# A four-layer graph network on one core: where the layer steps stand among the attention groups, the bank of the projection, and two node buffers instead of a copy

## The reference

```python
# layers 0, 2, 3: normalised adjacency times nodes times a 128x128 weight, plus bias (0 and 2 add the identity to adj)
x = _layernorm(x + (d[:, :, None] * adj * d[:, None, :]) @ x @ W + b)
# layer 1: additive attention
q = x @ WQ; k = x @ WK
score = einsum('bijd,d->bij', relu(q[:, None] + k[:, :, None]), p)
x = _layernorm(x + softmax(score + mask(adj > 0)) @ x)
```

## Time and profile before

| | |
|---|---|
| median of 3 runs | 13884.19 us (13881.76 to 13884.51) |
| the profiled execution, first to last instruction | 13883.0 us |
| busy share of the span | DVE 96%, PE 93%, ACT 93%, POOL 8% |
| a middle sweep, from its first mask to the next sweep's | 1699.6 us |

### The profile page before, as it was taken

The page is one execution under the profiler, slowest core; times in us unless marked ns, Lnnn a source line. Parts: engine busy times, 40 slices in busy tenths (PEclk is TensorE's granted clock), DMA queues, the critical chain, the costliest instruction groups (busy, mean ns, idle before and its releaser), DMA issues.

```text
span 13883.0 us, 318102 instructions
## 1 busy us (share of the span) xinstructions
PE 12956.7 (93%) x143877; PEld 5442.7 (39%) x143877; DVE 13327.1 (96%) x14041; ACT 12942.7 (93%) x8528; POOL 1095.3 (8%) x706
## 2 busy tenths in 40 slices
PE   7889989999899999999999998999989999899988
PEld 3333434443344333444334443344434444333333
DVE  7999999999999999999999999999999999999995
ACT  6999999999999999999999999999999999999994
POOL 0000000010000100010000100001100010000000
PEclk9999999999999999999999999999999999999999
DMA  4111112221122112221122211222112221011103
GB/s 144 52 46 49 50 58 84 89 63 44 61 90 90 59 37 74 86 87 56 44 72 86 84 59 37 77 87 84 59 36 82 84 80 58 32 49 52 43 12 111
DMA packets 680284, 918.70 MB, mean 66 GB/s; under 512 B 60432, under 2 KB 421904, under 8 KB 659472
## 3 DMA queue, kind: packets, MB, share of 16 engines
q1 hardware_dynamic: 678928, 898.35, 20.7%
HBM read 705.23 MB, written 184.55 MB: 64 GB/s over the span
## 4 chain that ended last, share of the span: by engine, by line
DVE 56%; PE 34%; ACT 7%; issue 2%; DMA 1%; POOL 0%; SPq 0%; DVEq 0%; POOLq 0%; ACTq 0%
DVE big L1110 50%; PE score L1269 24%; ACT big L861 6%; PE acc L1183 5%; PE acc L1242 2%; PE turn L1154 2%; DVE att L1048 2%; DVE big L1090 1%; DVE gx L997 1%; DMA piece<-adj_turned 0%; DVE gx L976 0%; PE turn L1213 0%; DVE stats L984 0%; ACT q_pair L769 0%; DVE att L1037 0%
## 5 line engine op out<-in xcount | busy, mean ns | idle before, releaser
L1110 DVE TENSOR_SCALAR big<-q_pair,k_pair_cols 128x2048 f32<-128x2048 f32 x10029 | 12094.2, 1278 | 289.8 <-PE score L1269 272.4
L861 ACT ACTIVATE big<-q_f,k_cols 128x2048 f32<-128x2048 f32 x6060 | 11633.5, 1998 | 256.9 <-PE score L1269 247.5
L1269 PE MATMUL score<-big,unit_window 128*32 128x512 f16 x82592 | 5439.0, 394 | 750.3 <-DVE big L1110 716.7
L1269 PE MATMUL score<-big,sign_window 128*32 128x512 f32 x48480 | 5591.5, 595 | 69.2 <-ACT big L861 67.5
L1269 PEld LDWEIGHTS score<-big,unit_window 128*32 128x32 bf16 x82592 | 2308.1, 96 | 3952.0 <-DVE big L1110 1128.8
L1269 PEld LDWEIGHTS score<-big,sign_window 128*32 128x32 f32 x48480 | 1572.3, 110 | 3299.2 <-issue 2948.4
L1183 PE MATMUL acc<-piece,q_f 128*128 128x512 f32 x2944 | 1411.5, 602 | 18.1 <-DVE q_f L959 10.7
L668 POOL TENSOR_SCALAR att_var<-att_mom 128x1 f32<-128x1 f32 x128 | 73.4, 573 | 9809.0 <-DVE att_mom L1066 9809.0
L1183 PEld LDWEIGHTS acc<-piece,q_f 128*128 128x128 f32 x2944 | 503.1, 190 | 529.8 <-issue 470.2
L1242 PE MATMUL acc<-x,att_turned 128*128 128x128 f32 x4096 | 559.4, 280 | 0.0
L1242 PEld LDWEIGHTS acc<-x,att_turned 128*128 128x128 f32 x4096 | 504.1, 194 | 56.8 <-issue 56.8
(11 more groups left out here) (95 smaller groups left out, 2876.3 us busy)
## 6 DMA issues: line engine op xcount, KB each, us to landing
piece<-adj_turned SPq DMA_DIRECT2D x1472, 256.0 KB, 2.7
att<-in_adj_dram SPq DMA_DIRECT2D x128, 1024.0 KB, 5.2
q_pair<-in_adj_dram SPq DMA_DIRECT2D x240, 512.0 KB, 4.5
adj_turned<-q_pair SPq DMA_DIRECT2D x224, 512.0 KB, 4.8
adj_turned<-big SPq DMA_DIRECT2D x16, 1024.0 KB, 13.5
q_f<-in_adj_dram SPq DMA_DIRECT2D x16, 512.0 KB, 5.4
gx<-in_x_dram SPq DMA_DIRECT2D x32, 256.0 KB, 4.0
q_kept<-q_pair SPq DMA_DIRECT2D x32, 256.0 KB, 3.7
```

What stands on the lines that cost most here:

```text
L861: ins = nc.scalar.activation(ring["A"][:, RANK[g] % RING * 4 + u, :], q_of(c + 1), ACT.Relu, bias=k_cols[:, t % 2, QUAD * u + g:QUAD * u + ...
L1110: ins = nc.vector.tensor_scalar(ring["D"][:, RANK[g] % RING * 4 + u, :], pairs_of(c + 1), k_pair_cols[:, t % 2, QUAD * u + g:QUAD * u + g ...
L1269: ins = nc.tensor.matmul(score[QUAD * u:QUAD * (u + 1), cc, :], (unit_window if pair else sign_window)[:, QUAD - 1 - g:2 * QUAD - 1 - g], ...
```

## The change

The twelve layer steps of a sweep no longer have a block each. Each has an end (`STEP_END`), 32 to 38 groups after the one before. The first piece of a sweep stands at place 38 in place of 60, the last step ends at place 454 in place of 444. The 16 pieces of a step are dealt evenly over the slots between the end of the step before (plus four groups) and its own, so two or three stand in each slot; the self product stands with the 14th piece. Eviction and projection stand at the end, the sum 3 or 4 groups behind, the root 5 and the output 12 behind, the bias 8 ahead. Queries and keys follow layer 0's steps at the next slots. GpSimd's extra row moves with the sum. A unit's two sums by ScalarE are put back to five groups behind an end where they would fall in between.

In the sweeps the projection writes `acc[1]`, the bank that the pieces used and that has been evicted, and the first piece of the next step waits for the sum to have read it (`layer_summed`). The waits on `acc_free` in the projection and on `layer_summed` in `weigh` go away.

`x1` and `gx` become two buffers, `nodes_of(b)` by the batch's parity. The layers of batches `c` and `c + 2` use one and the attention of `c + 1` the other, so `keep_x1` and its waits go away. `load_x2` is split: three quarters at place 28, once the last block's nodes have been read, the last at place 34. VectorE scales layer 2's nodes at places 31, 33, 35, 37 in place of 39, 44, 49, 54.

```diff
-    BLOCK = {"layer2": 2, "layer3": 6, "layer0": 10}
-    PIECES_AT = {-4: [0, 1, 2], 0: [3, 4, 5], 1: [6], 4: [7], 10: [8, 9], 14: [10], 18: [11], 23: [12, 13, 14, 15]}
-    SELF_AT, TURNED_AT, PROJECT_AT, SUM_AT, ROOT_AT, NORM_OUT_AT, STORE_AT = 18, 28, 28, 31, 33, 40, 41
-    SCALE_AT = {"layer2": [-25, -20, -15, -10], "layer3": [-5, -3, -1, 11], "layer0": [-5, -3, -1, 16]}
...
+    STEP_END = {"layer2": [70, 106, 142, 174], "layer3": [210, 247, 279, 316], "layer0": [352, 384, 422, 454]}
+    FIRST_PIECE_AT = 38
+    ALL_SLOTS = [t * GROUPS + at for t in range(T) for at in SLOTS]
...
+    def slots_of(k):
+        first = FIRST_PIECE_AT if k == 0 else ENDS[k - 1] + 4
+        return [at for at in ALL_SLOTS if first <= at < ENDS[k]]
+
+    PIECE_PLACE = {(name, s): [slots_of(n * STEPS + s)[i * len(slots_of(n * STEPS + s)) // T] for i in range(T)]
+                   for n, name in enumerate(LAYERS) for s in range(STEPS)}
...
+    ROOT_AFTER, NORM_OUT_AFTER, STORE_AFTER, X0_AFTER, BIAS_BEFORE, LOAD_BEFORE = 5, 12, 13, 17, 8, 4
+    SCALE_PLACE = {"layer2": [31, 33, 35, 37],
+                   "layer3": [STEP_END["layer2"][-1] + at for at in (-1, 1, 3, 15)],
+                   "layer0": [STEP_END["layer3"][-1] + at for at in (-1, 1, 3, 20)]}
...
+    def qk_places(s):
+        at = {"turn": slot_from(STEP_END["layer0"][s] + 17)}
...
-        x1 = sb("x1", [P, T, D])
-        gx = sb("gx", [P, T, D])
+        nodes_bufs = [sb(f"nodes_{i}", [P, T, D]) for i in range(2)]
...
+        def layer_acc(c):
+            return acc[0 if one_of(c, OPENING, CLOSING) else 1]
...
+            def load_x2(c, s):
+                sp.wait_ge(acc_free, block_of(c, 0) + AHEAD)
                 for i in range(2):
...
-            def keep_x1(c):
...
-                sp.dma_start(x1[:], gx[:]).then_inc(x1_ready, 16)
...
                 if i == 0:
                     pe.wait_ge(layer_turned, step_of(c, name, s) + AHEAD)
+                    if not one_of(c, OPENING) and (not one_of(c, CLOSING) or (name, s) == ("layer2", 0)):
+                        pe.wait_ge(layer_summed, step_of(c, name, s))
...
-                elif not one_of(c, OPENING):
-                    pe.wait_ge(acc_free, block_of(c, BLOCK[name] + s) + AHEAD)
                 for j in range(PER):
-                    ins = nc.tensor.matmul(acc[0][:, j * P:(j + 1) * P], y_turned[:, j * P:(j + 1) * P], w_sb[name][:],
-                                           start=True, stop=True)
+                    ins = nc.tensor.matmul(layer_acc(c)[:, j * P:(j + 1) * P], y_turned[:, j * P:(j + 1) * P],
+                                           w_sb[name][:], start=True, stop=True)
...
-                for name, s in steps_at(c, place, SELF_AT):
-                    if name != "layer3":
+                for name, s, i in pieces_at(c, place):
+                    if i == T - PER + 1 and name != "layer3":
                         add_self(c, name, s)
```

More of the change, by code:

```diff
@@ L72, in build @@
-    X1_AT, X2_AT, X0_AT = 28, 34, 45
+    LAYERS = ("layer2", "layer3", "layer0")
+    STEP_END = {"layer2": [70, 106, 142, 174], "layer3": [210, 247, 279, 316], "layer0": [352, 384, 422, 454]}
+    FIRST_PIECE_AT = 38
+    ALL_SLOTS = [t * GROUPS + at for t in range(T) for at in SLOTS]
+    ENDS = [STEP_END[name][s] for name in LAYERS for s in range(STEPS)]
+    assert all(end in ALL_SLOTS for end in ENDS)
+    def slots_of(k):
+        first = FIRST_PIECE_AT if k == 0 else ENDS[k - 1] + 4
+        return [at for at in ALL_SLOTS if first <= at < ENDS[k]]
@@ new lines, in build, with slot_from, sum_offset @@
+    PIECE_PLACE = {(name, s): [slots_of(n * STEPS + s)[i * len(slots_of(n * STEPS + s)) // T] for i in range(T)]
+                   for n, name in enumerate(LAYERS) for s in range(STEPS)}
+    PROJECT_TIME = 5
+    def slot_from(place):
+        return min(at for at in ALL_SLOTS if at >= place)
+    def sum_offset(end):
+        return 4 if end % GROUPS == 0 else 3
+    SUM_PLACE = {(name, s): STEP_END[name][s] + sum_offset(STEP_END[name][s]) for name in LAYERS for s in range(STEPS)}
+    ROOT_AFTER, NORM_OUT_AFTER, STORE_AFTER, X0_AFTER, BIAS_BEFORE, LOAD_BEFORE = 5, 12, 13, 17, 8, 4
@@ L73, in build @@
+    QK = [qk_places(s) for s in range(STEPS)]
+    X2_AT, X2_LAST_AT = 28, 34
     DIAG_AT, DEGREE_AT, DIS_AT, KEEP_AT = 9 * GROUPS - 16, 9 * GROUPS + 8, 9 * GROUPS + 9, 11 * GROUPS + 9
@@ L274, in pool_rows, with sum_row_group @@
             return max(c * T + (T + t - 1), 0)
-        SUM_ROW = (30, 3)
+        SUM_ROW_PART = 3
         def sums_at(c, t):
-            return steps_at(c, t * GROUPS + SUM_AT, SUM_AT)
+            return [(name, s) for name in side_layers(c) for s in range(STEPS) if SUM_PLACE[name, s] // GROUPS == t]
         def has_sum_row(c, t):
             return len(sums_at(c, t)) > 0
+        def sum_row_group(c, t):
+            return [SUM_PLACE[step] % GROUPS - 1 for step in sums_at(c, t)]
         def sum_rows(c, t):
@@ L342, in qk_at @@
                 return []
-            return [s for s in range(STEPS) if place == start_of("layer0", s) + QK[what]]
+            return [s for s in range(STEPS) if place == QK[s][what]]
         def slot_place(k):
@@ L352, in sum_place @@
             k = 2 * u
-            return k // len(SLOTS) * GROUPS + SUM_UNIT[SLOTS[k % len(SLOTS)]]
+            at = k // len(SLOTS) * GROUPS + SUM_UNIT[SLOTS[k % len(SLOTS)]]
+            return max([end + PROJECT_TIME for end in ENDS if end < at < end + PROJECT_TIME], default=at)
         def units_where(c, holds):
@@ L551, in side @@
                     load_raw(c, 0)
-                for name, s in steps_at(c, place, FIRST_LOAD_AT):
-                    if s == 0 and not one_of(c, OPENING):
+                for name in side_layers(c):
+                    if place == LOAD_PLACE[name] and not one_of(c, OPENING):
                         if name == "layer0":
@@ L559, in side @@
                             load_piece(c, name, 0, i)
[L560 to L566, removed]
+                for name, s, i in pieces_at(c, place):
+                    i += PIECES
+                    if s + i // T < STEPS and not one_of(c, OPENING):
+                        load_piece(c, name, s + i // T, i % T)
+                for name, s in steps_at(c, place, STORE_AFTER):
                     if name == "layer3":
@@ L569, in side @@
                         sp.dma_start(out[c, s * BANK:(s + 1) * BANK, :].rearrange("(t p) f -> p t f", p=P),
-                                     gx[:, s * PER:(s + 1) * PER, :]).then_inc(out_stored, 16)
+                                     nodes_of(c)[:, s * PER:(s + 1) * PER, :]).then_inc(out_stored, 16)
                 if "layer2" in side_layers(c):
[L572 to L575, removed]
+                    for s in range(STEPS):
+                        if place == (X2_LAST_AT if s == STEPS - 1 else X2_AT):
+                            load_x2(c, s)
                 if "layer0" in side_layers(c):
@@ L635, in _ @@
                 side(OPENING, place)
-            keep_x1(FIRST)
             load_k(FIRST, 0)
@@ L710, in side @@
             def side(c, place):
-                for name, s in steps_at(c, place, ROOT_AT):
+                for name, s in steps_at(c, place, ROOT_AFTER):
                     layer_root(c, name, s)
@@ L826, in side @@
                     sum_unit(c, u)
-                for name, s in steps_at(c, place, TURNED_AT):
+                for name, s in steps_at(c, place, 0):
                     turn_layer(c, name, s)
@@ L1193, in project @@
                 n = step_of(c, name, s)
-                if n > 0:
+                if one_of(c, OPENING, CLOSING) and n > 0:
                     pe.wait_ge(layer_summed, n)
```

109 lines of the change are left out of this document (57 added, 52 removed).

## The result

The changed kernel takes 14057.78 us (median of 4 runs, 14046.65 to 14064.59) against 13882.98 (4 runs, 13880.62 to 13884.51): ratio 1.0125, 95% interval 1.0111 to 1.0139. It is 175 us slower. I had forecast slower, but by 60 us, and 14058 lies outside my range. The profiled execution has a span of 14051.2 us.

A forecast was written before the change was run, and what follows sets the result against it. VectorE was taken to bound a block up to row 4 and mostly TensorE from there to group 24. 13883.0 + 54 (six middle sweeps) + 9 (LAST) + 2 (FIRST) - 5 (copy, load) = 13943 us, range 13775 to 14010.

The forecast's parts named there:

- F1: VectorE's part of a block, from its release by TensorE to row 4: 36.6 us before, 35.5 bare plus its VectorE items.
- rival C: TensorE idles longer ahead of group 4 and its clock falls: 64 us on top, 14007 us; chance 0.13.
- I take 9, the middle: A middle sweep gets longer by 4.5 to 13.8 us; 9 taken, so +54 for six sweeps.
- high routes: Upper bound for blocks 1 to 13: row 9 is waited for anew, later bursts and VectorE may bind; sum 1404 us.
- low routes: Lower bound for blocks 1 to 13: TensorE runs without a gap from row 4, or VectorE's length; sum 1394 us.
- copy and buffers: The x1 copy gone ahead of FIRST gives back 3 us, the split load 2: together -5.
- the first piece's wait on the sum: The piece's new wait is covered, at no cost; bare it would be 1.1 us a step, 92 us in the sweeps.
- the shared bank: The wait of projection against norm at place 27 goes away, worth nothing.
- the split load: Three quarters of x2 load before the last store in CLOSING: between nothing and 4.0 us gained, 2 taken.
- A: Rival: TensorE bounds the whole block, so the spread pays, 1.2 us less per block, -100, 13785 us; chance 0.25.
- B: Rival: no change, moved stops only trade places; 13880 us with the small savings; chance 0.20.
- The signs I named: Longest blocks 1, 8, 10, 11; gap from row 9 to ahead of group 4; group 11 stop over 2 us; idleness 45 to 54.

The follow-up runs named there:

- e3: The changed kernel with its ends, bank and buffers, but the pieces dealt by the old weights, thick ahead of row 4: 13885.85 us, 1.0003 of the kernel before.
- e6: The changed kernel with all pieces and self products of slot 6 two groups earlier, at place 4: 13940.71 us, 1.0039 of the kernel before.
- e4: The changed kernel with four more unread 128x128 products ahead of each of groups 3 and 4, filling TensorE's gap: 13989.97 us, 1.0079 of the kernel before.
- e12: The changed kernel with slot 6's pieces at slot 4 and, in group 10, the unit turned ahead of the weights: 13916.06 us, 1.0024 of the kernel before.
- e13: The kernel before with only the order in group 10 changed, the unit turned ahead of the attention weights: 13862.14 us, 0.9986.
- e14: The changed kernel's ends, bank and buffers with the old slot weights, and the unit turned first in group 10: 13865.16 us, 0.9989 of the kernel before.
- e9: The kernel before with pieces 8 and 9 moved from slot 10 to 4 and 6, and the unit turned first in group 10: 13778.53 us, 0.9925.
- e2: The kernel before with pieces 8 and 9 moved from slot 10 to places 4 and 6, nothing else: 13835.65 us, 0.9969.
- e1: The kernel before with the two node buffers and the split load only: 13881.05 us, 0.9999.
- e7: The changed kernel with GpSimd's extra row in the next VectorE group at or behind the sum: 14075.74 us, 1.0137 of the kernel before.

## Why the prediction was wrong

**What bounds it, right in the main.** VectorE leads from group 24 to row 4, TensorE mostly from there on. Work ahead of row 4 is cheap and work behind it isn't: e3 (the same steps, spread, dealt to the hidden slots) loses nothing, e6 gets 117 us back by two groups of place. VectorE's part F1 changes as I reckoned: in the third stretch it is 35.9 us (5606.98 to 5642.92) in place of 36.6 (5766.65 to 5803.28), 0.7 less; 1.16 less for the sum and 0.6 more for the bias that now stands there are 0.56 less.

**The step that failed: the sum left the clock out.** I had it as rival C, an alternative with 0.13, and summed on rows at full clock. But it doesn't compete with the routes, it comes on top of them: the same moved pieces make TensorE idle ahead of row 4. The fillers of e4, which change nothing else, gave back 68 of the 175 us. My argument against it, that idleness ahead of group 4 need not reach the part that counts, is refuted by the rows: the low stretch begins 0.87 us after row 4 starts and lies on rows 4 and 5, where TensorE has just taken the lead. C's size was good: 1.4 us in half of the blocks, 64 us; the rows show 1.66 us in 50 blocks, 83 us, and 68 came back with e4.

**The second: "I take 9, the middle".** Without the low clock (e4) the 13 stretches are 1405.45 us; my high routes sum to 1404, the low ones to 1394. They fall so: 109.7, 107.2, 107.6, 106.5, 109.7, 107.4, 107.4, 109.0, 107.1, 107.7, 108.5, 109.6, 108.0. In nine of the 13 that is within 1.3 us of the high route; in blocks 3, 5 and 12 it is 1.4 to 2.5 more, in 9 it is 1.6 less. So the number of the high routes fits, but their mechanism isn't shown. In them VectorE, stopped behind slots 10 and 14, is late for row 20. It is stopped (2.28, 2.43 us), yet in the third stretch TensorE then never waits for it, and in the fifth it waits 1.61 us for row 17, behind three scalings and a sum on VectorE:

```profile
5905.18 2.00 PE L1303 MATMUL score<-big,unit_window 128*32 128x512 f16 x32 [1.61 <-DVE big L1148]
```

Over the trace its waits ahead of row 20 even fell, from 68.8 to 54.0 us. That the sums agree is then in part luck. In part it is luck too that e12's 1395.07 is near the low routes' 1394: its block 11 takes 106.8 us and was to take 109.8, block 13 takes 108.0 and was to take 105.7.

Had I taken the high routes (13.8 a sweep, so 83, and as much for sweep LAST), the sum would be 13977; with the 68 us of the clock it is 14045, against 14058. So of the 115 us between forecast and measurement 68 are the clock and 34 the routes. The last 13 are met by what lies behind block 13: the six middle sweeps got 154 us longer, 140 of it in the 13 stretches and 14 behind them. 10 of these are in block 14, where the last step now ends and for which my sum had no term. LAST itself got longer by 16 us (1560.5, was 1544.6, mask to mask), not 9, and FIRST by 1.7, as I said.

**The route that was not in the model.** ScalarE's rows had no place in it. In the kernels here it is worth 20 to 25 us (e13, e14, e12) and 57 where the other route is shortened (e9). It made little of the error of the forecast, since it stands in both kernels with nearly the same worth (e13 20 us, e12 25), but it made e2's expectation wrong by half.

**What I costed at nothing or little.** Right: copy and buffers (e1, within 0.1%; I had put -5), the first piece's wait on the sum and the shared bank (in e3, nothing). No wait for `nodes` in the sweeps appears, so the scalings at place 31 are covered. The wait for q_pair ahead of the first sweep fell from 11.4 to 9.4 us: 2, I took 3. The 2 us that I gave the split load are not to be seen: after the last sweep VectorE waits 7.7 us for nodes in the trace, 5.3 before. Not foreseen was that TensorE would wait for GpSimd's row (62.5 us in all), but e3 has it at no loss and e7 moves it at no gain. Why e7 is 18 us slower stays open; so do the extra 1.4 to 2.5 us of blocks 3, 5 and 12. The waits seen there in e4 are 0.90 us for GpSimd's row in block 3 and 1.56 us for row 17 in block 5, terms that my sum lacked; no run takes them away alone.

**The rivals.** A (the spread pays) is refuted: with the deal of before the spread is worth nothing (e3), since block 14 takes what the others give. It decides, I wrote, if two groups of ring carry TensorE's lateness past group 24; the stops of 2.28 and 2.43 us say that they don't. B (places don't matter) is refuted by 172 us between e3 and the changed kernel, with the same work. The Trainium skill's rule beside B (Perfetto Trace Analysis, Identifying the Most-Contended Engine) would see no difference: VectorE is at 95 to 96%, TensorE's weight loads at 39% in either. The trace disagrees: what moved 1.2% of the time (172 us) was when TensorE does its side work.

**The signs I named.** Longest were blocks 5, 8, 1 and 12 (I said 1, 8, 10 and 11); 3 and 6 grew, 13 did not. The gap went from row 9 to row 4. VectorE's stop of over 2 us came, but behind groups 6 and 14, not 11. Behind slot 23, where the third and the fifth stretch leave two pieces (1.88 us at 5707.64 and 5925.55), VectorE does not stop; that was right. VectorE's idleness was to be 45 to 54 us and is 64.5. Block 1 left 104.3: 110.0, and 108.61 in e12, which is my 4.3 us more.

## What to carry over

Where two engines take turns at the lead, side work has a price by its place: look for the gap of the one that follows and put the work into it, not behind it, and not evenly. Count what a step costs in every block that it reaches, the last one too. Work taken out of the idle time ahead of such a place is paid twice: once where it goes, and once because TensorE's first work behind the longer gap can run at the low clock (here behind 61 of 115 such gaps). Add that to the sum; it is no alternative to it. And draw the route of every engine that feeds the ring (here ScalarE too) before pricing a move: a cure of one route shows only when the next one is shortened as well.

## What was not expected of the hardware

On a TensorE that was otherwise nearly always at work, a gap of 2.23 us (5858.76) and one of 2.78 us (5642.92) are each followed by 3.4 us at half clock, and 50 blocks with layer work have such a low stretch near row 4 (the one at 0.54 is shown above). The length of the gap alone doesn't decide: one of 2.80 us is followed by full clock, and so are 54 of the 115 gaps of 2 us or more ahead of row 4. In the block shown of before, a gap of 1.73 us left the whole stretch at 1.00, though 17 others had their low clock near row 9. Work that nobody reads, 2.3 us of it in the gap, made the kernel 68 us faster.
